# Second-level routing and dispatch of a two-level mixture layer, as one loop over the first-level groups

## The reference, cut to what matters

```python
xn = _l2norm(x) * scale * gamma_in                 # layer stage of the kernel
logits1 = einsum('bGgd,esd->bGges', xg, phi)       # 128 rows x (8 groups x 16 slots)
disp1, comb1 = softmax(logits1, 2), softmax(logits1 over all 128 slots)
slots = einsum('bGgd,bGges->bGesd', xg, disp1)
yn = _l2norm(slots) * scale * gamma2               # stored by the layer stage as yn
means = yn.reshape(b, G, E1, m, ns, d).mean(axis=4)            # 4 means of 4 slots each
se2 = _l2norm(einsum('bGkmd,kdf->bGkmf', means, w_slot2)) * scale   # 4 experts x 4, per group k
logits2 = einsum('bGksd,bGkemd->bGksem', yn, se2)  # 16 slots x 16, per block and group
disp2 = softmax(logits2, axis=3); comb2 = softmax(logits2 over the 16)
slots2 = einsum('bGksd,bGksem->bGkemd', yn, disp2) # what the experts read
...                                                # 32 experts, then
out2 = einsum(o, comb2); out = einsum(out2, comb1) # comb2 and comb1 are multiplied ahead: combT
```

## Time and profile before

| | us |
|---|---|
| median of 3 runs | 3242.74 |
| the runs | 3239.6 to 3253.91 |
| the profiled execution | 3253.83, span 3252.0 |
| routing, first DMA issue to dispatch's first | 180.4 |
| dispatch, to the experts' first DMA issue | 220.6 |
| PE busy over the span | 2958.8 (91%) |
| granted clock of PE, mean | 0.969 |

### The profile page before, as it was taken

How to read it: one execution, slowest core, us unless ns; L and a number is a source line. 1 busy time by engine, 2 the same in 40 slices (tenths; PEclk the granted TensorE clock), 3 DMA queues, 4 the chain that set the end, 5 groups by cost and what they waited for, 6 DMA issues and landing times. The chain is left out here.

```text
span 3252.0 us, 63751 instructions
## 1 busy us (share of the span) xinstructions
PE 2958.8 (91%) x21571; PEld 2841.3 (87%) x21571; DVE 1908.7 (59%) x3165; ACT 1540.4 (47%) x3998; POOL 1444.2 (44%) x1406
## 2 busy tenths in 40 slices
PE   3999999999999999999999757788899999999986
PEld 3899999999999999999999747688899999999983
DVE  4456565565656565656555457455676766666754
ACT  3354545455454545454545334355454444454530
POOL 0334344444444343434444447200466766666650
PEclk9999999999999999999999979899999999999998
DMA  4001001010101010100101056455666666666869
GB/s 123 29 23 44 24 31 37 24 44 24 44 24 44 24 44 23 43 24 29 38 24 39 28 230 271 132 169 156 200 210 205 197 190 185 209 192 193 261 225 362
DMA packets 293655, 359.10 MB, mean 110 GB/s; under 512 B 24328, under 2 KB 285960, under 8 KB 293512
## 3 DMA queue, kind: packets, MB, share of 16 engines
q1 hardware_dynamic: 284840, 344.92, 33.0%
q10 hardware_dynamic: 8704, 12.58, 1.0%
HBM read 286.14 MB, written 71.30 MB: 110 GB/s over the span
## 5 line engine op out<-in xcount | busy, mean ns | idle before, releaser
L1611 PE MATMUL u_bank<-x_in,x_w 128*128 128x256 f32 x4608 | 585.4, 286 | 27.9 <-issue 17.4
L1611 PEld LDWEIGHTS u_bank<-x_in,x_w 128*128 128x128 f32 x4608 | 578.8, 195 | 30.3 <-issue 30.3
L929 POOL TENSOR_TENSOR hT_lo<-h_tmp,hT_hi 128x512 fp32r<-128x512 f32 x192 | 247.8, 1291 | 471.0 <-DVE hT_hi L817 471.0
L1764 POOL TENSOR_TENSOR x_w<-raw,x_w 128x768 fp32r<-128x768 f32 x128 | 274.1, 2141 | 296.2 <-DVE x_w L1707 296.2
L1768 POOL TENSOR_TENSOR x_aT<-x_act,x_aT 128x512 fp32r<-128x512 f32 x128 | 299.3, 2338 | 217.2 <-ACT x_aT L1676 217.2
L390 PE MATMUL m_bank<-yT_hi,w_hi 128*128 128x256 f32 x1152 | 339.7, 295 | 0.0
L1667 ACT ACTIVATE x_gelu<-u_bank,x_b1T 128x256 f32<-128x256 f32 x256 | 121.3, 474 | 444.8 <-PE u_bank L1611 444.8
L390 PE MATMUL m_bank<-yT_lo,w_hi 128*128 128x256 f32 x1152 | 324.5, 282 | 0.0
L390 PE MATMUL m_bank<-yT_hi,w_lo 128*128 128x256 f32 x1152 | 323.7, 281 | 0.0
L663 ACT ACTIVATE h_tmp<-m_bank,b1c 128x256 f32<-128x256 f32 x384 | 160.6, 470 | 330.1 <-PE m_bank L390 329.7
L1623 PE MATMUL o_bank<-x_w,x_aT 128*128 128x384 f32 x1536 | 289.6, 336 | 1.8 <-POOL x_aT L1768 1.8
(11 more groups left out here) (213 smaller groups left out, 7343.0 us busy)
## 6 DMA issues: line engine op xcount, KB each, us to landing
raw<-in_L_ffn_w_dram SPq DMA_DIRECT2D x384, 384.0 KB, 5.0
ws_raw<-in_L_ffn_w_slot_dram SPq DMA_DIRECT2D x8, 2304.0 KB, 9.4
x_in<-in_x_dram SPq DMA_DIRECT2D x32, 384.0 KB, 3.5
x_res<-in_x_dram SPq DMA_DIRECT2D x32, 384.0 KB, 4.2
residual<-f_sb SPq DMA_DIRECT2D x32, 384.0 KB, 2.5
yn<-yn_sb SPq DMA_DIRECT2D x32, 384.0 KB, 2.5
yk<-yn SPq DMA_DIRECT2D x16, 768.0 KB, 11.1
se<-se SPq DMA_DIRECT2D x16, 768.0 KB, 3.3
```

The costliest lines, as they stand in the source:

```text
L929: nc.gpsimd.tensor_tensor(hT[i % 3][1][:], h_tmp[i % 2][:], hT[i % 3][0][:].bitcast(F32), ALU.subtract).then_inc(hl.sem, 1)
L1611: mm = pe.matmul(u_bank[n % BANKS][:, g, :], w1s[i % 2][a][:, c, g, c2 * P:(c2 + 1) * P], xT[e % 2][b][:, c, :], start=c == 0 and j == 0, ...
L1764: nc.gpsimd.tensor_tensor(w2s[i % 2][1][:], raw2[i][:], w2s[i % 2][0][:].bitcast(F32), ALU.subtract).then_inc(w2_lo.sem, 1)
```

## The change

`routes` is gone and `dispatch` does both. A tile of 128 rows is no longer one block with all its 8 groups, but one group (k) with its 16 slots in 8 blocks; 8 tiles make a group, and the mask's 16 x 16 squares stand for blocks instead of groups. `body(n, d, t, par)` does three things side by side: routing of group n, dispatch of group d = n - 1, and loading and transposing of group t = n + 1. There are ten such passes, written out in `over_groups`.

- yn is read once; the transposed tiles ynT serve the logits and also the means, which DVE sums from ynT (`sums`) already transposed. POOL's adds and PE's transposes of the means go.
- se2 no longer goes to DRAM: the scaled rows are transposed (`route_T`) and copied into seT in SBUF, every fourth element.
- The weights come in four pieces (one per expert) in two buffers instead of a whole group at once; DVE makes their low halves, ACT the high ones. POOL does the addition of eps and the power, nothing else but the mask.
- comb1T and combT are moved a tile at a time, 8 blocks x 16 slots, 64 KB each.
- logits, exponentials and norms go over 4 tiles at once (512 wide), transposed logits return to the bank the logits were in; slot rows have one bank.
- `free_semaphores()` with its barrier stands ahead of the stage.

Cut to its core (the removed functions are in the kernel before):

```diff
-        with ExitStack() as ctx:
-            routes(nc, ctx, sb, ps, sem, ident, nhalf, eps, f_w_slot2, yn_dram, se_dram)
+        free_semaphores()
...
+    yn = [sb(ctx, f"d_yn{i}", [P, NJ, D]) for i in range(2)]
+    ynT = [sb(ctx, f"d_ynT{i}", [P, DC, NJ, P]) for i in range(2)]
+    seT = sb(ctx, "d_seT", [P, DC, NB, M2, E2])
+    se = [sb(ctx, f"d_se{i}", [P, D]) for i in range(2)]
+    raw = [sb(ctx, f"ws_raw{i}", [P, DC, D]) for i in range(2)]
+    ws = [[sb(ctx, f"ws_{i}_{s}", [P, DC, D], F32R) for s in range(2)] for i in range(2)]
+    msum = sb(ctx, "m_sum", [P, DC, NB * M2 // HB])
+    mT = [[sb(ctx, f"mT_{i}_{s}", [P, DC, P], F32R) for s in range(2)] for i in range(HB)]
...
+    t_bank, s_bank, w_bank, o_bank = (ps(ctx, f"d_{n}_bank", [P, 512]) for n in "tswo")
+    g_bank = [ps(ctx, f"d_g_bank{i}", [P, 512]) for i in range(2)]
+    l_bank = [ps(ctx, f"d_l_bank{t}", [P, 512]) for t in range(HB)]
...
+    def turn_bank(j):
+        return l_bank[0] if j % 2 else t_bank
+
+    def over_groups(eng, body):
+
+        body(None, None, 0, 1)
+        body(0, None, 1, 0)
+        body(1, 0, 2, 1)
+        with eng.Fori(0, (E1 - 4) // 2) as h:
+            body(2 * h + 2, 2 * h + 1, 2 * h + 3, 0)
+            body(2 * h + 3, 2 * h + 2, 2 * h + 4, 1)
+        body(E1 - 2, E1 - 3, E1 - 1, 0)
+        body(E1 - 1, E1 - 2, None, 1)
+        body(None, E1 - 1, None, 0)
...
+            def load_yn(t, par, *js):
+                for j in js:
+                    if past(t, 2):
+                        sp.wait_ge(o_full.sem, o_full.at(t - 2, j + 1))
+                    sp.dma_start(yn[1 - par][:, j, :], yn_dram[8 * j:8 * j + 8, bass.ds(t * S1, S1), :].rearrange(
...
+            def load_cb(d, t):
+                if past(d, 1):
+                    sp.wait_ge(c_full.sem, c_full.at(d - 1, t + 1))
+                for j in range(JT):
+                    b = 8 * (t * JT + j)
+                    sp.dma_start(cb[t][:, j, :], comb_dram[b:b + 8, bass.ds(d * S1, S1), :].rearrange("b s d -> b (s d)")
+                                 ).then_inc(cb_landed[t].sem, 16)
...
+            def body(n, d, t, par):
+                R, O, T = n is not None, d is not None, t is not None
+                if R: load_ws(n, 2); load_ws(n, 3)
+                if R and not O: load_cb(0, 0); load_cb(0, 1)
+                if O and R: load_cb(d + 1, 0)
+                if O: store_ct(d, 0)
+                if T: load_ws(t, 0)
+                if T: load_yn(t, par, 0, 1, 2, 3)
+                if O and R: load_cb(d + 1, 1)
+                if O: store_ct(d, 1)
+                if T: load_ws(t, 1)
+                if T: load_yn(t, par, 4, 5, 6, 7)
...
+                e, i = divmod(v, HB)
+                pe.wait_ge(wl.sem, wl.at(n, e + 1))
+                pe.wait_ge(ml.sem, ml.at(n, i + 1))
+                if v >= 2:
+                    pe.wait_ge(se_ok.sem, se_ok.at(n, v - 1))
+                elif past(n, 1):
+                    pe.wait_ge(se_ok.sem, se_ok.at(n - 1, NV - 1 + v))
+                for c in range(DC):
+                    for q, (a, b) in enumerate(((0, 0), (0, 1), (1, 0))):
+                        mm = pe.matmul(g_bank[v % 2][:, 0:D], mT[i][a][:, c, :], ws[e % 2][b][:, c, :],
+                                       start=c == 0 and q == 0, stop=c == DC - 1 and q == 2)
...
+            def logits(d, par, t):
+                if d is None:
+                    return
+                pe.wait_ge(seT_ok.sem, seT_ok.at(d, NV - 1 + t))
+                if t == 0 and not (isinstance(d, int) and d == E1 - 1):
+                    pe.wait_ge(yT_ok.sem, yT_ok.at(d + 1, NJ))
+                if past(d, 1):
+                    pe.wait_ge(cex_ok.sem, cex_ok.at(d - 1, JT * (t + 1)))
...
+                pe.wait_ge(nm_ok.sem, nm_ok.at(d, t + 1))
+                if t:
+                    pe.wait_ge(ct_ok.sem, ct_ok.at(d, 1))
+                elif past(d, 1):
+                    pe.wait_ge(ct_ok.sem, ct_ok.at(d - 1, HB))
...
+            def body(n, d, t, par):
+                logits(d, par, 0); route(n, 0); logits_T(d, 0); logits(d, par, 1); route(n, 1)
+                disp_T(d, 0); route_T(n, 0); logits_T(d, 1); route(n, 2); back(d, 0); rows(d, par, 0)
+                route_T(n, 1); rows(d, par, 1); route(n, 3); disp_T(d, 1); rows(d, par, 2); route_T(n, 2)
+                rows(d, par, 3); route(n, 4); back(d, 1); rows(d, par, 4); route_T(n, 3); rows(d, par, 5)
+                route(n, 5); rows(d, par, 6); route_T(n, 4); rows(d, par, 7); route(n, 6)
+                turn(t, par, 0); route_T(n, 5); turn(t, par, 1); route(n, 7); turn(t, par, 2); route_T(n, 6)
...
+                means(n, 1); row_exps(d, 0); square(n, 0); col_exps(d, 0); square(n, 1); disp_T(d, 0); row_exps(d, 1)
+                ws_high(n, 2); col_exps(d, 1); square(n, 2); rows(d, 0); rows(d, 1); square(n, 3); disp_T(d, 1)
+                rows(d, 2); ws_high(n, 3); rows(d, 3); square(n, 4); rows(d, 4); rows(d, 5); square(n, 5); rows(d, 6)
+                ws_high(t, 0); rows(d, 7); square(n, 6); turn(t, par, 0); turn(t, par, 1); square(n, 7)
+                turn(t, par, 2); turn(t, par, 3); ws_high(t, 1); turn(t, par, 4); turn(t, par, 5); means(t, 0)
+                turn(t, par, 6); turn(t, par, 7)
...
+            def sums(t, par, i):
+                dve.wait_ge(yT_ok.sem, yT_ok.at(t, JT * (i + 1)))
+                if i:
+                    dve.wait_ge(ml.sem, ml.at(t, 1))
+                elif past(t, 1):
+                    dve.wait_ge(ml.sem, ml.at(t - 1, HB))
+                nc.vector.tensor_reduce(msum[:], ynT[1 - par][:, :, i * JT:(i + 1) * JT, :].rearrange(
+                    "p c j (q s) -> p c (j q) s", s=NS), X_AXIS, ALU.add).then_inc(ms_ok.sem, 1)
...
+            def route_T(n, v):
+                dve.wait_ge(s_full.sem, s_full.at(n, v + 1))
+                if past(n, 1):
+                    dve.wait_ge(l_full.sem, l_full.at(n - 1, i + 1))
+                nc.vector.tensor_copy(seT[:, :, 32 * i:32 * i + 32, :, e].rearrange("p c b m -> p c (b m)"),
+                                      s_bank[:, 0:D].rearrange("p (c q) -> p c q", c=DC)).then_inc(seT_ok.sem, 1)
...
+            def norms(d, t):
+                if d is None:
+                    return
+                dve.wait_ge(ex_ok.sem, ex_ok.at(d, JT * (t + 1)))
+                dve.wait_ge(cex_ok.sem, cex_ok.at(d, JT * (t + 1)))
...
+                sums(n, 1 - par, 1); logits(d, 0); means(n, 1); col_max(d, 0); scale(n, 0); norms(d, 0); logits(d, 1)
+                scale(n, 1); route_T(n, 0); col_max(d, 1); scale(n, 2); ws_low(n, 2); back(d, 0); route_T(n, 1); norms(d, 1)
+                scale(n, 3); route_T(n, 2); ws_low(n, 3); scale(n, 4); back(d, 1); route_T(n, 3); scale(n, 5); route_T(n, 4)
+                ws_low(t, 0); scale(n, 6); route_T(n, 5); scale(n, 7); route_T(n, 6); sums(t, par, 0); ws_low(t, 1); route_T(n, 7)
+                means(t, 0)
...
+            def power(n, v):
+                if n is None:
+                    return
+                pool.wait_ge(sq.sem, sq.at(n, v + 1))
+                nc.gpsimd.tensor_tensor(ms[:, 1, v:v + 1], ms[:, 0, v:v + 1], eps[:, 0:1], ALU.add).then_inc(ve.sem, 1)
+                pool.wait_ge(ve.sem, ve.at(n, v + 1))
+                nc.gpsimd.tensor_tensor(ms[:, 2, v:v + 1], ms[:, 1, v:v + 1], nhalf[:, 0:1], ALU.pow).then_inc(rs.sem, 1)
```

More of the change, by code:

```diff
@@ L985, in run, with dispatch @@
     body(None, None, NG - 1, None)
-def routes(nc, ctx, sb, ps, sem, ident, nhalf, eps, w_slot2, yn_dram, se_dram):
+def dispatch(nc, ctx, sb, ps, sem, ident, nhalf, eps, w_slot2, yn_dram, comb_dram, ct_dram, slots2T):
+    NJ = NB // 8
     HB = 2
[L994 to L1023, removed]
@@ new lines, in back, with rows @@
+            def back(d, t):
+                if d is None:
+                    return
+                pe.wait_ge(cb_landed[t].sem, cb_landed[t].at(d, 16 * JT))
+                pe.wait_ge(dT_ok.sem, dT_ok.at(d, t + 1))
+                for j in range(JT):
+                    mm = pe.matmul(w_bank[:, j * P:(j + 1) * P], lg[t][:, j, 0, :], cb[t][:, j, :], start=True, stop=True)
+                mm.then_inc(c_full.sem, 1)
+            def rows(d, par, j):
+                if d is None:
+                    return
+                if j % JT == 0:
+                    pe.wait_ge(dT_ok.sem, dT_ok.at(d, j // JT + 1))
+                if j:
+                    pe.wait_ge(o_ok.sem, o_ok.at(d, j))
+                elif past(d, 1):
+                    pe.wait_ge(o_ok.sem, o_ok.at(d - 1, NJ))
+                for c in range(DC):
+                    mm = pe.matmul(o_bank[:, c * P:(c + 1) * P], yn[1 - par][:, j, c * P:(c + 1) * P], dT[j // JT][:, j % JT, :],
+                                   start=True, stop=True)
+                mm.then_inc(o_full.sem, 1)
@@ L1102, in body @@
-            def body(k, j, h, nxt):
-                for n in range(NP):
-                    i, e = divmod(n, E2)
-                    act.wait_ge(full.sem, full.at(k, n + 1))
```

(23 more changed lines are left out.)

565 lines of the change are left out of this document (200 added, 365 removed).

## The result

The changed kernel takes 3211.3 us (median of 4, 3204.8 to 3217.1) beside 3244.5 (3239.6 to 3253.9): a ratio of 0.9894, 95% interval 0.9864 to 0.9924, so 33 us less. The profiled execution took 3217.1 us, its span 3215.3. The range of the prediction holds it, but by luck: the windows by stage say something else than the prediction did.

What follows compares the result with a forecast made beforehand. Routing and dispatch were taken as bound by PE plus waits between its pieces; the fused stage, summed over ten passes and a barrier, took 384.8 against 401.0 us, so 3242.7 - 16.2 = 3226.5 us, range 3205 to 3257.

Steps and rivals of the forecast that it cites:

- The experts ... I cost them at nothing.: Experts and combination behind the rewritten stage: not touched, reading the same slots2T and combT, so 0 us of change.
- The reference of 401.0 us: Routing (180.4 us) plus dispatch (220.6 us) in the profiled kernel before, the length the new stage was compared with.
- the walk: One full turn of the fused loop laid out on paper: 34.6 us of PE work plus 10.9 of waits, 45.5 us.
- The sum of the stage: Fused stage: passes of 13.7, 28.3, six of 45.5, 43.3 and 25.7 us, with the barrier 384.8, 16 us less.
- heavier rival: Fused stage: sums at half rate (stage 411 us) or clock dropping to 0.85 (stage 401); 3236 to 3254, chance 0.18.
- The longest stop: PE before the second disp_T in each turn, waiting 3.2 us for DVE's norms(d,1), queued behind scale(n,2).
- the clock of 0.93: PE's granted clock in the fused stage, taken as 0.93, making 32.2 us of work a turn 34.6.
- PE never waiting for a DMA after the first pass: Sign in the fused loop that DMAs have slack; waits of 5 us a turn would mean the slower rival.
- slower rival: Fused loop's transfers too slow: at 150 GB/s a turn 50.3 us, stage 427, 26 us more, about 3268; chance 0.10.
- The prices: DVE's instructions in the fused stage: low half 1.38 us, sums 1.76, scaling 0.64, copy into seT 1.0.
- The lines of 16 bytes: DVE's copy into seT: crossing SBUF lines costs, 1.0 us taken; at 0.55 the stage would be 7 us shorter.
- The lighter rival: Fused stage with plain-copy price into seT and full PE clock: turn 43.5, stage 368, 33 us less, about 3209; chance 0.22.

Runs made afterwards that it cites:

- early waits: Kernel before with 164 or 80 already met TensorE waits at setup's start, moving the experts loop's code: 3211.1 us (0.9897) and 3214.3 us (0.9899).
- sixth run: Changed kernel with g2's scaling moved behind the second half's norms on VectorE, and SyncE's weights' and later yn loads ahead of comb's loads and combT's stores: 3166.9 us, 0.9756.
- fourth run: Changed kernel with one edit in VectorE's order, the scaling of g2 put behind the normalising of the second half: 3191.8 us, ratio 0.9845.
- eleventh run: Changed kernel with only SyncE's order changed, weights' load and four later yn loads ahead of comb's loads and combT's stores: 3198.2 us, 0.9858.
- seventh run: Changed kernel with seT laid out so VectorE's copy writes neighbouring elements and TensorE reads the logits' operand at a distance: 3240.5 us, 0.9983.

## Why the prediction came out, and why its reason did not

The forecast was 16 us less, from the fused loop; 33 came, from elsewhere. That the time lies in the range is luck: the gain that was forecast did not come, and one that no case had took its place. Point by point:

- **"The experts ... I cost them at nothing."** This step failed. The path of the data into them is indeed the same, but the change moved their code, and that was worth 36 us in the profiled pair, 30 to 33 by the medians with early waits. No case of the prediction had it. The lines that would have warned were in the page before: queue 8 with 84 packets, and a stop in each pass of a loop that is otherwise always busy.
- **The reference of 401.0 us** was one execution, the longest of five; the mean is 392.6. Against that the walk's 384.8 was a gain of 8, not 16. I had seen that the execution stood 11 us above the median, and did not ask in which stage.
- **The sum of the stage**, 384.8, against 392.7, 395.6 and 389.6. By pieces in the changed kernel, from one group's first logits to the next's: ahead of the first full turn 46.5 (walked 42.0), six turns 46.4 each (45.5), the next 40.2 (43.3), the end 27.6 (26.5 with the barrier). Close, but TensorE's own work was too low and its waits too high: 37.7 us busy a turn at clock 0.93 (walked 34.6) and 8.7 standing (10.9). At clock 1.00, in the sixth run, a turn still has 34.3 us of work, where the pieces summed to 32.2. Two slips are in the paper sums: the waits at the bank of the rows, 1.8 + 3 x 0.5, are 3.3 and not 3.4 (the 10.9 has it right), and at a clock of 0.85 the heavier rival's turn is 32.2/0.85 + 10.9 = 48.8, not 47.5, its stage some 407 and not 401.
- **The longest stop**, before the second disp_T with VectorE's norm as its releaser: 2.6 us, walked 3.2, and its cause, the scaling ahead of it that waits for a square behind the weights' cast, is as the fourth run shows. The clock of 0.93 came out as taken.
- **"PE never waiting for a DMA after the first pass"** failed: 17 waits, 14.5 us, of which 1.9 us in a full turn, not the 5 that were named as the slower rival's sign. I had the room and the flight of the last yn tile, but not SyncE's queue, in which it stood behind eight issues of some 0.8 us; with SyncE's order changed (eleventh run) the waits of the full turns were gone. Of the slower rival only this much is true; the transfers were not short of bandwidth (102 GB/s asked, 0.36 of the engines busy).
- **The prices**: low half 1.35 (1.38), sums 1.74 (1.76), scaling 0.62 (0.64), copy into seT 0.84 (1.0 taken, bounds 0.55 and 1.0). The row of ScalarE's spaced read, double the price an element, led too high for VectorE's write, which costs half as much again (0.84 against 0.55). The lines of 16 bytes of the Trainium skill (SBUF — State Buffer, "Door 1: The DMA port swizzle"), of which it says that crossing to another is paid for, bear on it, and the seventh run agrees that there is a cost. Its saving was named as 7 us of the stage; no run tests that, since the seventh changed TensorE's read with it.
- **The lighter rival** was named with 3209, where the time lies. It was right by number only: neither of its conditions, the cheap copy and the full clock in the stage, held. With its stops taken out the stage gets there (347 us, clock 1.00 in the turns): that the clock goes with the stops, I had down only as a loss of the heavier rival, not as a reward for mending them.

## What to carry to other kernels

Before crediting a change with what an untouched stage gains or loses, look at the instruction packets of the page and at the pass length of that stage's loop: a TensorE loop of some 1600 instructions can cost 7% more or less by where its code begins, and any edit ahead of it moves it. Move it with met waits where the engine stands anyway (80 at the setup's start did here), and compare both kernels at the cheap place. Take the reference of a stage from several executions, not one. And where a turn has several stops, look at the granted clock with each that is mended: here it went from 0.93 to 0.94 and 0.97 with one and to 1.00 with both, and the shorter busy time that went with it was as much as the standing time won.

## What the runs showed of the hardware

- A TensorE loop of 1611 instructions ran without any instruction packet at offsets of 80 and 164 instructions from where the kernel before has it, and with nine packets and 5 to 9.5 us more a pass at offsets of 0 and 256. A loop of 881 instructions (the layer's) had none in any of these runs.
- An instruction of two waits that are met already cost TensorE 0.11 us (18 us for 164, 28 us for 256).
- TensorE was busy 0.23 us with each record of a logits matmul (128 columns, f32) whose columns come from four rows 1 KB apart in turn, and 0.15 us with neighbouring ones, at the same granted clock of 0.91.
- VectorE's copy of 128x384 f32 out of PSUM took 0.84 us when it wrote every fourth element and 0.55 us when it wrote neighbours.
- Two executions of the same code differ by up to 14 us in a stage of 390 (clock 0.89 to 0.93) and by 8.6 us in when the layer ends.
